# A two-layer recurrent model in one kernel: zeros of a parked image written from a tile on chip, large products of a block inversion moved to GpSimd, the first two heads inverted on TensorE, and a new order of all work

## The chip, the cores and the metric

One core of a Trainium2 chip runs the whole program in one launch. The metric is the device time of that launch in microseconds. Engines are called TensorE (PE in the rows, PEld for its weight loads), VectorE (DVE), ScalarE (ACT), GpSimd (POOL) and SyncE (SP), which issues nearly all DMAs here.

## The reference

Two layers over x of shape (2, 512, 256). Layer 0 multiplies causal attention (16 heads of 16) with silu of a mixture of 8 experts. Layer 1 is the larger part: 16 key heads, each with two value heads, a delta rule with decay, and beside it a mixture with 2 shared and 16 routed experts (top 2). Cut to what matters:

```python
def step(state, inp):                      # layer 1, for each token t
    q_t, k_t, v_t, b_t, d_t = inp
    Sk = jnp.einsum('bhi,bhipj->bhpj', k_t, state)
    delta = (v_t - Sk) * b_t[..., None]
    upd = jnp.einsum('bhi,bhpj->bhipj', k_t, delta)
    state = state * d_t[:, :, None, :, None] + upd
    o = jnp.einsum('bhi,bhipj->bhpj', q_t, state)
    return (state, o)
...
s = _L1_attn_ref(xn, ...)                  # conv of 4 taps, the scan, rmsnorm, silu(z), W_out
g = _silu(_L1_ffn_ref(xn, ...))
x = x + s * g
```

## The kernel before

**Chunks.** The scan is done in chunks of 128 tokens. A unit u (0 to 63) is one chunk i of one key head h, u = 4h + i, for both batches and both value heads: four lanes of 128x128. Inside a chunk the delta rule needs the inverse of a lower triangular 128x128 matrix, one for each lane. The kernel inverts it by doubling: from the inverses of the diagonal blocks of width w those of width 2w are made.

**The steps of a unit**, by the names of the plan: `row` and `dec` fetch and build the decays (RC, E; SP, GpSimd, ScalarE), `gram` multiplies keys and queries (TensorE L1580) and masks them on VectorE (L2200: M for the inverse, PTE for the output), `pl` and `pm` (GpSimd L2754, L2758, L2760) split M into a high and a low 16-bit part in the tile LM and put ones on the diagonal. `ls` stores LM into an image in memory called `parked` (two buffers, one for each second head), `ps` and `pd` take PTE through memory to transpose its place.

**The inner blocks, once for each head.** When the four units of a head are parked, `dg` loads their 16x16 diagonal blocks into LC (eight DMAs), so that each partition holds blocks of its own. `iv1`, `iv2`, `iv3` invert them there on VectorE in sixteen small instructions; the last four are a product of 512 elements (L1909, `times_left`), a sum (L2223), a product of 512 (L1915, `times_right`) and a sum (L2229). ScalarE copies the result and its transpose to 16 bits (`xc`), and `sx` stores it back into the image in sixteen DMAs (L1253). The rest of the image's inverse planes must be zero: that is what the two `blank` transfers of the start are for.

**The outer levels, for each unit.** `ld` loads the unit's inverse, its transpose and its matrix, high and low (XYLM, three buffers, L1260). Then for levels k = 5, 6, 7: `a` (TensorE L1591, four matmuls of 64 columns, then VectorE L2238 masks into ZL) and `b` (TensorE L1600 and L1603, eight such matmuls, then ScalarE L2516 writes back into XYLM). `r` and `c` refine the result once and give W (VectorE L2244, L2252). The state recurrence follows: `KS`, `U`, `so` (TensorE L1630, L1646, L1660), normalisation `sq`, `on`, gating `ot`, and the output products `os`, `ol`, `y`, `yl`.

**Other work** fills the engines: the projections and the convolution of the next heads (`ck`, `cq`, `cv`, `Zt`: products L1307 on TensorE, taps L2116 on VectorE), `fWK`, `fWV`, `fWO` (weights, split by GpSimd into a high and a low part), the routing (`top`, `cnt`, `own`, `tiles`, `hits`) and the experts.

**Order.** Every engine runs a fixed list in order. The lists come from a planner at build time (`Plan.arrange`): each part has an engine, a cost and the parts it comes after; of the parts ready, the one with the earliest start (in steps of `GRAIN`) goes first, and ties go by a rank. `RANK` and `LATER` shift ranks and starts for each kind of part and engine; they were searched.

**The start of the program.** SP fetches weights; the transfers of the small inputs (`fetch_small`) all count on one semaphore:

```python
for k in range(2):
    sp.dma_start(parked[k, 0:2].rearrange("k p q t -> k p (q t)").bitcast(U16),
                 A["blank"].unsqueeze(0).broadcast_to((2, 128, 2048))).then_inc(d_l1, 16)
...
elif x[0] == "spg":                       # GpSimd: the split of wab (L2586, L2588)
    w.wait_ge(d_l1, 96)
```

`spg` stands in GpSimd's list between splits of expert weights (`fx`, tiles exh and exl). Behind it come two `fWK` and three `fx`.

Of the kernel before, what the change touches and what calls it, by code (L numbers as in the profile page):

```python
# [18 lines left out]
D = 256  # L19
NT = 8  # L20
C_ID, C_SEL, C_U, C_ONE, C_LV = 0, 128, 256, 384, 512
LEVELS = range(5, 8)
C_IO = C_LV + 3 * 64
# [12 lines left out]
def constants():  # L36
# [21 lines left out]
def later_keys():  # L58
# [16 lines left out]
    "KS": {"ACT": -190.92, "DVE": -1855.73, "PE": -624.17}, "KS:first": {"ACT": 227.91, "DVE": -29.25, "PE": 1091.89},  # L75
    "KS:last": {"ACT": 19.9, "DVE": -251.47, "PE": -182.36}, "U": {"ACT": 271.82, "PE": -704.74},
    "U:first": {"ACT": 522.41, "PE": -459.55}, "U:last": {"ACT": 1098.98, "PE": 26.26},
    "Vt": {"ACT": 1966.37, "PE": 1.01}, "Vt:first": {"ACT": -177.22, "PE": 116.15},
    "Zt": {"ACT": -442.91, "DVE": 372.72, "PE": 0.27}, "Zt:first": {"ACT": -6.92, "DVE": -918.91, "PE": 0.43},
    "a": {"DVE": 745.93, "PE": -37.51}, "a:first": {"DVE": 7.23, "PE": -43.11},  # L80
    "a:last": {"DVE": 219.97, "PE": -2044.99}, "am:0": {"POOL": -319.97}, "am:1": {"POOL": -358.83},
    "b": {"ACT": 1147.73, "PE": -216.88}, "b:first": {"ACT": -284.84, "PE": -11.2},
    "b:last": {"ACT": 1292.06, "PE": -123.68}, "c": {"DVE": 139.61, "PE": -193.02},
    "c:first": {"DVE": 5.13, "PE": -513.63}, "c:last": {"DVE": -88.29, "PE": 203.76},
    "cb": {"DMA": 35.71, "DVE": -174.03, "POOL": -432.42}, "ck": {"ACT": -69.56, "PE": -8.56}, "ck1": {"DVE": -77.72},
    "ck1:first": {"DVE": -32.49}, "ck2": {"DVE": 1249.32}, "ck2:first": {"DVE": -735.45}, "ck3": {"DVE": 2346.47},
    "ck3:first": {"DVE": 71.49}, "ck:first": {"ACT": 60.74, "PE": -13.19}, "cnt": {"DVE": 69.46, "PE": 259.48},
    "cq": {"ACT": -622.29, "PE": 0.48}, "cq1": {"DVE": 113.6}, "cq1:first": {"DVE": -39.01}, "cq2": {"DVE": 2640.45},
    "cq2:first": {"DVE": 206.34}, "cq3": {"DVE": -540.73}, "cq3:first": {"DVE": 677.48},
    "cq:first": {"ACT": -297.9, "PE": -14.62}, "crow": {"ACT": 48.35, "PE": -275.28, "SP": 352.22},  # L90
# [3 lines left out]
    "dd:1": {"SP": 438.02}, "dec": {"ACT": -84.12, "POOL": -63.05}, "dec:first": {"ACT": 152.18, "POOL": -5.94},  # L94
    "dec:last": {"ACT": -310, "POOL": -684.57}, "dg": {"SP": -106.09}, "dg:first": {"SP": -251.24},
# [2778 lines left out]
```

## Time and profile before

| | us |
|---|---|
| median of 3 runs | 1363.14 |
| lowest, highest | 1357.52, 1367.53 |
| the profiled execution | 1364.12 |
| its span, first to last instruction | 1362.4 |

| engine | busy us | share of the span |
|---|---|---|
| TensorE | 1173.1 | 86% |
| TensorE, weight loads | 981.3 | 72% |
| VectorE | 1101.6 | 81% |
| ScalarE | 833.0 | 61% |
| GpSimd | 823.1 | 60% |

The share is a mean over stages: layer 0 (to about 280 us), the prologue and the filling of layer 1's pipeline (to about 450), the steady part over 16 heads, and the tail. Matmuls are pipelined and their ends are modelled, so TensorE's busy time is not its peak. The profile also gives the clock that TensorE was granted, as a share of full speed, here 0.946 in the mean.

### The profile page before, as it was taken

The numbers are of one execution on the slowest core, as the hardware profiler recorded it, in microseconds if no ns is written. First come the engines' busy times: TensorE is split into PE (matmuls) and PEld (weight loads), VectorE is DVE, ScalarE is ACT, GpSimd is POOL, SyncE is SP. The second block draws the span as 40 slices with busy tenths as digits, with TensorE's granted clock in tenths as the row PEclk, the third lists the DMA queues.
The fourth block names the chain that finished last, engine by engine and source line by source line (L and its number), as shares of the span: only waits on it lengthen the run. The fifth ranks groups of instructions, "written<-read, shape, count | busy, mean of one in ns | idle before, by whom it ended". The sixth has DMA issues, their size and how long they took to land.

```text
span 1362.4 us, 28169 instructions
## 1 busy us (share of the span) xinstructions
PE 1173.1 (86%) x9546; PEld 981.3 (72%) x9546; DVE 1101.6 (81%) x2393; ACT 833.0 (61%) x2377; POOL 823.1 (60%) x1052
## 2 busy tenths in 40 slices
PE   9890997979288899899889998999998999988996
PEld 7560544658177788879778887888886888877885
DVE  6790523698889889798988898899888988977888
ACT  4000364267266677677757785777776677857675
POOL 3111244255765587777587776876776778666636
PEclk9895798989699999999999998999999999989998
DMA  7931011315354364653566444644463654554442
GB/s 224 234 110 56 16 53 40 96 62 143 87 165 128 97 163 126 172 156 108 140 155 188 111 128 114 176 116 141 107 196 86 171 151 134 138 128 122 132 123 67
DMA packets 236871, 172.41 MB, mean 127 GB/s; under 512 B 116824, under 2 KB 204120, under 8 KB 236696
## 3 DMA queue, kind: packets, MB, share of 16 engines
q1 hardware_dynamic: 231992, 156.32, 42.0%
q0 software_dynamic: 4736, 14.29, 3.9%
q8 instruction: 77, 1.26, 0.4%
q14 instruction: 66, 0.54, 0.1%
HBM read 121.93 MB, written 50.52 MB: 127 GB/s over the span
## 4 chain that ended last, share of the span: by engine, by line
PE 28%; DVE 24%; DMA 20%; SPq 9%; POOL 8%; issue 7%; ACT 4%; DVEq 0%; POOLq 0%; ACTq 0%
PE ps L1307 10%; DMA XYLM<-parked 6%; SPq L1253 4%; DMA parked<-LM 4%; DMA parked<-in_blank 3%; SPq L1245 3%; DVE yv L2116 3%; DVE KQ L2116 2%; DVE PR L1909 2%; DVE PR L1915 2%; DMA RC<-crow 2%; DMA LC<-parked 2%; POOL LM L2758 1%; DMA parked<-XY 1%; DVE M L2200 1%
## 5 line engine op out<-in xcount | busy, mean ns | idle before, releaser
L2116 DVE SCALAR_TENSOR_TENSOR KQ<-ps,cw,KQ 128x511 f32<-128x511 f32 (+2 forms) x192 | 141.2, 743 | 6.6 <-ACT KQ L2452 4.1
L2116 DVE SCALAR_TENSOR_TENSOR yv<-ps,cw,yv 128x511 f32<-128x511 f32 (+2 forms) x192 | 142.5, 744 | 3.5
L2516 ACT ACTIVATE XYLM<-ps 128x512 f16<-128x512 f32 x192 | 111.2, 598 | 52.5 <-PE ps L1603 49.7
L1307 PE MATMUL ps<-XH,WVh 128*128 128x256 f32 (+1 forms) x384 | 135.6, 353 | 4.6 <-ACT QSc L2525 2.0
L2550 ACT ACTIVATE sq<-O 128x128 bf16<-128x128 f32 x256 | 79.3, 310 | 75.5 <-DVE O L2288 32.1
L1307 PE MATMUL ps<-XH,WVl 128*128 128x256 f32 (+1 forms) x384 | 124.2, 324 | 0.0
L1307 PE MATMUL ps<-XL,WVh 128*128 128x256 f32 (+1 forms) x384 | 124.1, 323 | 0.0
L2238 DVE TENSOR_TENSOR ZL<-ps,cst 128x256 f16<-128x256 f32 x192 | 78.0, 418 | 20.8 <-PE ps L1591 17.3
L2744 POOL TENSOR_TENSOR RC<-RC,dec 128x512 f32<-128x512 f32 x64 | 67.7, 1057 | 32.1 <-DMA RC<-crow 31.9
L2556 ACT ACTIVATE O<-O,small 128x128 f32<-128x128 f32 x256 | 82.4, 410 | 3.0 <-POOL small L2770 2.6
L1995 DVE TENSOR_REDUCE Mp<-ps 128x2 f32<-128x768 f32 (+2 forms) x64 | 48.8, 816 | 43.0 <-PE ps L1387 42.8
L2380 ACT ACTIVATE hT<-ps 128x512 f32<-128x512 f32 x16 | 9.6, 598 | 120.7 <-PE ps L1307 120.7
L2789 POOL TENSOR_TENSOR OGL<-O,OGH 128x512 fp32r<-128x512 f32 x62 | 80.2, 1294 | 5.1
L1307 PEld LDWEIGHTS ps<-XH,WVh 128*128 128x128 f32 x384 | 74.1, 193 | 10.4 <-ACT QSc L2525 2.7
L1630 PE MATMUL ps<-S,KQ 128*128 128x256 f32 x192 | 62.4, 407 | 20.8 <-DVE O L2288 13.4
L2758 POOL TENSOR_TENSOR LM<-M,LM 128x512 f16<-128x512 f32 x64 | 76.6, 1198 | 5.2
L1660 PEld LDWEIGHTS ps<-De,PT 128*128 128x128 f32 x512 | 74.4, 191 | 6.3 <-ACT De L2541 0.9
L1307 PEld LDWEIGHTS ps<-XH,WVl 128*128 128x128 f32 x384 | 73.6, 192 | 6.0
L1660 PE MATMUL ps<-De,PT 128*128 128x128 f32 x512 | 77.1, 275 | 0.8 <-ACT De L2541 0.6
L1307 PEld LDWEIGHTS ps<-XL,WVh 128*128 128x128 f32 x384 | 74.3, 194 | 3.8
L2538 ACT ACTIVATE D<-ps,dec 128x128 f32<-128x128 f32 x192 | 60.8, 376 | 25.2 <-PE ps L1646 24.9
L1591 PE MATMUL ps<-XYLM 128*128 128x64 f16 x768 | 51.5, 195 | 27.2 <-DMA XYLM<-parked 24.6
(341 smaller groups left out, 4123.5 us busy)
## 6 DMA issues: line engine op xcount, KB each, us to landing
XYLM<-parked SPq DMA_DIRECT2D x64, 512.0 KB, 5.4
RC<-crow SPq DMA_DIRECT2D x128, 128.0 KB, 4.8
decayed<-PTE SPq DMA_DIRECT2D x64, 256.0 KB, 4.4
PT<-decayed SPq DMA_DIRECT2D x64, 256.0 KB, 3.3
parked<-LM SPq DMA_DIRECT2D x64, 256.0 KB, 3.5
WV<-in_WV SPq DMA_DIRECT2D x16, 512.0 KB, 3.7
exr<-in_ex SPq DMA_DIRECT2D x16, 384.0 KB, 5.9
WK<-in_WK SPq DMA_DIRECT2D x16, 256.0 KB, 2.9
```

What stands on the lines that cost most here:

```text
L1307: m = pe.matmul(o, a, b, start=c + k == 0, stop=c == 1 and k == 2)
L1630: pe.matmul(ps[:, bk, 0:256], K[:, h % 3, 128 * n:128 * n + 128], S[:, b], start=True, stop=True)
L1660: m = pe.matmul(ps[:, bk, 256 + 128 * v:384 + 128 * v], PT[:, u % 2, 2 * b + v, :], De[:, b, v, :], start=True, stop=True)
L2116: m = dve.scalar_tensor_tensor(out=dst[:, k:512], in0=ps[:, bk, 0:512 - k], scalar=cw[:, h, j, 3 - k:4 - k], in1=dst[:, k:512], op0=ALU.mu ...
L2238: leave(dve.tensor_tensor(half(ZL[:, k - 5], k, 0), p, lv(k), ALU.mult), "a", u, k)
L2516: leave(act.activation(changed(u, k), ps[:, bank("b", u, k), :].rearrange("p (c n t) -> p c n t", c=2, t=1 << (k - 1)), ACT.Copy), "b", u, k)
L2538: m = act.activation(D2[:, b, v, :], ps[:, bk, 128 * v:128 * v + 128], ACT.Copy, scale=bE[:, cl:cl + 1])
L2550: act.activation(sq[:, 1, :], O[:, u % 2, l, :], ACT.Square, accum_out=so[:, u % 2, l:l + 1]).then_inc(s_sqo, 1)
L2556: m = act.activation(O[:, u % 2, l, :], O[:, u % 2, l, :], ACT.Copy, scale=ro[:, u % 2, l:l + 1])
L2744: pool.tensor_tensor(rc.rearrange("p (b v) t -> p b v t", b=2), rc.rearrange("p (b v) t -> p b v t", b=2), bias.unsqueeze(3).broadcast_to( ...
L2758: pool.tensor_tensor(early(u, 1), M[:, u % 2], early(u, 0), ALU.subtract).then_inc(s_ml, 1)
L2789: pool.tensor_tensor(OGL[:], O[:, u % 2], OGH[:].bitcast(F32), ALU.subtract).then_inc(s_ogl, 1)
```

## The change

1. The zeros of the image come from a tile `blank` (128 x 512, 16 bits) that GpSimd clears at the start, in four DMAs of 512 KB with the 128 partitions outermost, instead of two DMAs of 1 MB from an input in memory with the two buffers outermost. All waits on the semaphore go from 96 to 128.
2. The two products of 512 elements of a head's inner blocks are issued by GpSimd (`p8`, `q8`) instead of VectorE; the sums stay.
3. The first two heads (`LEAD`, eight units, `OWN`) don't go through memory. GpSimd writes their masks straight into XYLM, adds the transposed first step (`py`) and the identity (`xi`), TensorE and VectorE do a first step `x1`, and the doubling runs from level 2 to 7 instead of 5 to 7. For them `ls`, `dg`, `iv`, `xc`, `sx` and `ld` fall away. The masks of levels 2 to 4 lie in a tile ZF that shares its place with XC and PR, so `iv1` of head 2 waits for level 4 of all eight units; `pl`, `py`, `xi` of unit u wait for the unit three before, since XYLM has three buffers.
4. The planner's costs of SP are the issue alone, and landings are parts of their own; `RANK` and `LATER` are new throughout, so all lists are in a new order.

```diff
-C_ID, C_SEL, C_U, C_ONE, C_LV = 0, 128, 256, 384, 512
-LEVELS = range(5, 8)
+C_ID, C_SEL, C_U, C_ONE, C_X1, C_Y1, C_LV = 0, 128, 256, 384, 512, 576, 704
+LEVELS = range(2, 8)
+OUTER = 5
+LEAD = 2
+OWN = 4 * LEAD
...
-    P.add(("pt", u), rank + 0.1, ("DVE", 0.79, (("gram", u), "DVE"), earlier(2, "ps", "SP")), gives=("gram", u))
-    P.add(("ps", u), rank + 0.2, ("SP", 1.0, (("pt", u), "DVE"), earlier(8, "pd", "SP")))
+    P.add(("pt", u), rank + 0.1, ("DVE", 0.79, (("gram", u), "DVE"), earlier(2, "ps", "DMA")), gives=("gram", u))
+    P.add(("ps", u), rank + 0.2, ("SP", 0.45, (("pt", u), "DVE"), earlier(8, "pd", "DMA")), ("DMA", 1.5))
+    if u < OWN:
+        rank = u - 1.5
+        P.add(("pl", u), rank, ("POOL", 0.6, (("gram", u), "DVE"), earlier(3, "c", "DVE"), earlier(3, "r", "PE")))
+        P.add(("pm", u), rank, ("POOL", 2.1, (("pl", u), "POOL")))
+        P.add(("py", u), rank + 0.1, ("POOL", 1.2, (("pm", u), "POOL")))
+        P.add(("xi", u), rank, ("POOL", 0.48, earlier(3, "r", "PE"), (("cc", 1), "POOL")))
+        P.add(("x1", u), rank + 0.2, ("PE", 0.12, (("pm", u), "POOL"), (("cc", 1), "POOL")),
+              ("DVE", 0.34, earlier(3, "r", "PE"), (("xi", u), "POOL")), takes=True, gives=("x1", u))
+        return
...
-    P.add(("iv2", h), rank + 0.1, ("DVE", 1.3, (("iv1", h), "DVE")))
-    P.add(("iv3", h), rank + 0.1, ("DVE", 1.3, (("iv2", h), "DVE")))
+    P.add(("p8", h), rank + 0.1, ("POOL", 1.15, (("iv1", h), "DVE")))
+    P.add(("iv2", h), rank + 0.1, ("DVE", 0.8, (("p8", h), "POOL")))
+    P.add(("q8", h), rank + 0.1, ("POOL", 1.15, (("iv2", h), "DVE")))
+    P.add(("iv3", h), rank + 0.1, ("DVE", 0.8, (("q8", h), "POOL")))
...
+        first_head = ExitStack()
+        ZF = sb("ZF", [128, 3, 4, 128], F16, scope=first_head)
+        first_head.close()
         XC = sb("XC", [128, 256])
         PR = sb("PR", [128, 512])
...
-                for k in range(2):
-                    sp.dma_start(parked[k, 0:2].rearrange("k p q t -> k p (q t)").bitcast(U16),
-                                 A["blank"].unsqueeze(0).broadcast_to((2, 128, 2048))).then_inc(d_l1, 16)
+                w.wait_ge(s_c0, 2)
+                for k in range(4):
+                    sp.dma_start(parked[k // 2, k % 2].rearrange("p (a q) t -> p a (q t)", a=4),
+                                 blank[:].unsqueeze(1).broadcast_to((128, 4, 512))).then_inc(d_l1, 16)
...
+                elif what == "x1":
+                    u = x[1]
+                    bk = enter(*x)
+                    w.wait_ge(s_const, 2)
+                    w.wait_ge(s_one, nth("POOL", "pm", u))
+                    for l in range(4):
+                        m = pe.matmul(ps[:, bk, 64 * l:64 * l + 64], xy(u, 2)[:, l, :], half(id16[:], 1, 0), start=True, stop=True)
+                    signal(m, *x)
...
                 elif what == "iv1":
                     h = x[1]
-                    w.wait_ge(d_dg, 128 * (h + 1))
-                    if h:
-                        w.wait_ge(s_xc, 2 * h)
-                    inner_blocks(IV * h)
+                    w.wait_ge(d_dg, 128 * (h - LEAD + 1))
+                    if h > LEAD:
+                        w.wait_ge(s_xc, 2 * (h - LEAD))
+                    else:
+                        for u in range(OWN):
+                            w.wait_ge(*full("b", u, OUTER - 1))
+                    inner_blocks(IV * (h - LEAD))
...
+                elif x[0] == "p8":
+                    h = x[1]
+                    w.wait_ge(s_iv, IV * (h - LEAD) + 12)
+                    times_left(pool, 8, 0, PR[:])
+                elif x[0] == "q8":
+                    h = x[1]
+                    w.wait_ge(s_iv, IV * (h - LEAD) + 14)
+                    times_right(pool, 8, 0, 0, PR[:])
                 elif x[0] == "pl":
                     u = x[1]
                     w.wait_ge(s_m, nth("DVE", "gram", u))
-                    if u > 1:
-                        w.wait_ge(d_ls[u % 2], 16 * ((u - 2) // 2 + 1))
+                    if u >= OWN + 2:
+                        w.wait_ge(d_ls[u % 2], 16 * ((u - 2 - OWN) // 2 + 1))
+                    elif 2 < u < OWN:
+                        w.wait_ge(*done("c", u - 3))
...
+                elif x[0] == "xi":
+                    u = x[1]
+                    w.wait_ge(s_const, 2)
+                    if u > 2:
+                        w.wait_ge(*full("r", u - 3))
+                    pool.tensor_copy(half(xy(u, 0), 1, 1), half(spread4(id16[:]), 1, 1)).then_inc(s_xi, 1)
+                elif x[0] == "py":
+                    u = x[1]
+                    w.wait_ge(s_one, nth("POOL", "pm", u))
+                    if u > 2:
+                        w.wait_ge(*done("c", u - 3))
+                    pool.tensor_tensor(xy(u, 1), xy(u, 2), spread4(cst[:, C_Y1:C_Y1 + 128]), ALU.mult).then_inc(s_y1, 1)
```

## Rows read from the trace of the kernel before

**Rows 1.** the page: TensorE and VectorE (busy us, share, instructions), TensorE by slices

```profile
PE 1173.1 (86%) x9546; PEld 981.3 (72%) x9546; DVE 1101.6 (81%) x2393; ACT 833.0 (61%) x2377; POOL 823.1 (60%) x1052
...
PE   9890997979288899899889998999998999988996
```

**Rows 2.** the chain that ended last, in order of time: start us, us, what

```profile
89.78 41.44 DMA parked<-in_blank
...
338.21 4.77 DMA parked<-LM
...
368.88 5.18 DMA XYLM<-parked
...
376.86 0.23 PE ps L1591 x4
...
378.96 0.29 PE ps L1591 x4
...
433.89 0.13 PE ps L1600 x4
```

**Rows 3.** the waits: engine line waited for, us in total, times, longest

```profile
POOL wabh L2586 <- DMA parked<-in_blank: 40.7, 1, 40.7
...
PE ps L1591 <- DMA XYLM<-parked: 24.6, 18, 2.3
...
PE ps L1530 <- issue: 23.5, 1, 23.5
...
PE ps L1630 <- DVE O L2288: 13.4, 11, 3.9
```

**Rows 4.** timeline near the pause: start us, us, engine, line, what

```profile
89.06 1.33 SPq L1113 DMA_DIRECT2D parked<-in_blank  x2
...
131.28 0.32 POOL L2586 CAST wabh<-wab 128x160 fp32r<-128x160 f32 x1 [40.73 <-DMA parked<-in_blank]
...
138.02 0.76 PE L1307 MATMUL ps<-XH,exh 128*128 128x512 f32 x1 [34.40 <-POOL exl L2588]
```

**Rows 5.** windows: stretch, length, engines busy, clock, DMA share, GB/s

```profile
core 0: us, PE busy (x) PEld busy (x) DVE busy (x) ACT busy (x) POOL busy (x), PEclk, DMA share, GB/s
88.00:92.00 4.00, 3.86 (x30) 2.52 (x30) 3.69 (x8) 0.00 (x0) 1.89 (x2) 1.00 1.06 314
104.00:131.00 27.00, 0.00 (x0) 0.00 (x0) 1.36 (x4) 0.00 (x0) 0.00 (x0) 0.52 0.12 54
131.00:160.00 29.00, 20.88 (x110) 12.22 (x114) 11.59 (x18) 7.75 (x11) 11.21 (x14) 0.62 0.03 7
335.00:380.00 45.00, 17.34 (x140) 14.21 (x139) 39.61 (x101) 14.84 (x38) 32.16 (x43) 0.70 0.48 130
335.00:600.00 265.00, 214.87 (x1868) 187.09 (x1868) 232.52 (x529) 169.26 (x513) 190.04 (x241) 0.94 0.50 135
600.00:1200.00 600.00, 556.62 (x4928) 493.26 (x4927) 538.22 (x1149) 434.95 (x1318) 434.15 (x552) 0.99 0.52 141
```

**Rows 6.** the page's DMA issues: times, KB each, median us from issue to landing

```profile
parked<-LM SPq DMA_DIRECT2D x64, 256.0 KB, 3.5
```

**Rows 7.** timeline of unit 0: its masks on GpSimd, its W on VectorE

```profile
317.43 0.61 POOL L2754 CAST LM<-M 128x512 f16<-128x512 f32 x1 [2.55 <-DVE M L2200]
...
383.24 0.68 DVE L2252 SCALAR_TENSOR_TENSOR W<-ps,XYLM 128x512 f32<-128x512 f32 x1
```

**Rows 8.** groups by form on TensorE: busy us, mean ns of one

```profile
L1600 PE MATMUL ps<-ZL,XYLM 128*128 128x64 f16 x768 | 54.2, 196 | 9.5 <-DVE ZL L2238 9.2
```

**Rows 9.** groups by form on VectorE and GpSimd

```profile
L2238 DVE TENSOR_TENSOR ZL<-ps,cst 128x256 f16<-128x256 f32 x192 | 78.0, 418 | 20.8 <-PE ps L1591 17.3 <-PE ps L1603 2.0 <-issue 0.9
...
L1915 DVE TENSOR_TENSOR PR<-XC,ZC 128x512 f32<-128x512 f32 x16 | 22.7, 1417 | 0.0
L1909 DVE TENSOR_TENSOR PR<-XC 128x512 f32<-128x512 f32 x16 | 19.5, 1218 | 0.2
...
L2758 POOL TENSOR_TENSOR LM<-M,LM 128x512 f16<-128x512 f32 x64 | 76.6, 1198 | 5.2
```

More of the change, by code:

```diff
@@ L74 @@
 RANK = {
[L75 to L90, printed above, removed]
[3 rows of a table removed]
@@ new lines @@
+    "sc:1": {"ACT": 0.5}, "sd": {"DVE": 0.15}, "slot": {"DVE": 0.08}, "small": {"SP": 0.53}, "so": {"DVE": 0.04},
+    "so:first": {"PE": 0.15}, "sq": {"POOL": 1.41}, "sq:first": {"ACT": 2.13, "POOL": 0.12},
+    "sq:last": {"ACT": 0.82, "POOL": 3.7}, "sr": {"DMA": 1.97, "POOL": 2.33}, "ss": {"SP": 0.87}, "su": {"ACT": 1.89},
+    "sw": {"DMA": 1.13, "POOL": 0.91}, "sx": {"DMA": 0.16}, "tiles": {"DVE": 3.89}, "tn0": {"DVE": 0.38},
+    "top": {"ACT": 0.01, "DVE": 1.9}, "tp": {"ACT": 1.34, "DVE": 1.51}, "up": {"ACT": 1.73}, "x1": {"DVE": 0.24},
@@ L179, with levels @@
-UNITS = ("row", "dec", "gram", "pt", "pl", "pm", "ls", "ps", "ld", "pd", "a", "b", "r", "c", "KS", "U", "so", "sq", "on", "ot", "os", "ol", "y", "yl")
+HEADS = ("ck", "ck1", "ck2", "ck3", "cq", "cq1", "cq2", "cq3", "cv", "cv1", "cv2", "cv3", "kn", "kb", "kns", "Vt", "Zt", "dg", "iv1", "p8", "iv2", "q8", "iv3", "xc", "sx")
+UNITS = ("row", "dec", "gram", "pt", "pl", "pm", "py", "xi", "x1", "ls", "ps", "ld", "pd", "a", "b", "r", "c", "KS", "U", "so", "sq", "on", "ot", "os", "ol", "y", "yl")
+def levels(u):
+    return LEVELS if u < OWN else range(OUTER, 8)
@@ L501, in plan_chunk @@
+    P.add(("pl", u), rank + 0.1, ("POOL", 0.6, (("gram", u), "DVE"), earlier(2, "ls", "DMA") if u > OWN + 1 else None))
     P.add(("pm", u), rank + 0.1, ("POOL", 2.1, (("pl", u), "POOL")))
-    P.add(("ls", u), rank + 0.2, ("SP", 1.0, (("pm", u), "POOL"), earlier(8, "ld", "SP")))
+    P.add(("ls", u), rank + 0.2, ("SP", 0.45, (("pm", u), "POOL"), earlier(8, "ld", "DMA") if u > OWN + 7 else None), ("DMA", 0.8))
 def plan_blocks(P, h):
     rank = 4 * h - 3.8
-    units = [(("ls", 4 * h + i), "SP") for i in range(4)]
@@ L508, in plan_blocks @@
-    P.add(("dg", h), rank, ("SP", 4.0, *units, (("iv1", h - 1), "DVE") if h else None))
-    P.add(("iv1", h), rank + 0.1, ("DVE", 2.5, (("dg", h), "SP"), (("xc", h - 1), "ACT") if h else None))
-    P.add(("iv2", h), rank + 0.1, ("DVE", 1.3, (("iv1", h), "DVE")))
-    P.add(("iv3", h), rank + 0.1, ("DVE", 1.3, (("iv2", h), "DVE")))
-    P.add(("xc", h), rank + 0.2, ("ACT", 0.9, (("iv3", h), "DVE"), (("sx", h - 1), "SP") if h else None))
-    P.add(("sx", h), rank + 0.2, ("SP", 8.0, (("xc", h), "ACT")))
+    units = [(("ls", 4 * h + i), "DMA") for i in range(4)]
@@ new lines, in plan_blocks @@
+    P.add(("dg", h), rank, ("SP", 4.0, *units, (("iv1", h - 1), "DVE") if h > LEAD else None), ("DMA", 0.3))
+    P.add(("iv1", h), rank + 0.1, ("DVE", 3.6, (("dg", h), "DMA"), (("xc", h - 1), "ACT") if h > LEAD else None,
+                                   *([(("b", k, OUTER - 1), "PE") for k in range(OWN)] if h == LEAD else [])))
+    P.add(("p8", h), rank + 0.1, ("POOL", 1.15, (("iv1", h), "DVE")))
+    P.add(("iv2", h), rank + 0.1, ("DVE", 0.8, (("p8", h), "POOL")))
+    P.add(("q8", h), rank + 0.1, ("POOL", 1.15, (("iv2", h), "DVE")))
@@ L665, in plan1 @@
         plan_chunk(P, u)
-    for h in range(HK):
+    for h in range(LEAD, HK):
         plan_blocks(P, h)
```

282 lines of the change are left out of this document (159 added, 123 removed), and 34 rows, old and new, of tables (LATER, RANK).

## The prediction

> **What bounds the kernel now.** I read the page first [rows 1]. TensorE is busy 86% of the span and VectorE 81%, and the row of slices has one hole: in the fourth slice (102 to 136 us) TensorE is at 0 and everything else nearly so. The page's chain of waits, in order of time [rows 2], names the hole: one piece of 41.44 us, the transfer of zeros into the parked image, which starts at 89.78. The waits [rows 3] say who stood there: GpSimd, 40.7 us, ahead of the split of wab (L2586), because that split waits for all six small loads and both zero transfers on one semaphore. GpSimd runs its list in order, and behind that instruction stand the splits of the experts' weights. So TensorE stops at 104 and starts again at 138.02 after 34.40 us [rows 4]. By stages [rows 5]: nothing runs in 104 to 131; from 335 to 380 TensorE is busy 17.3 of 45 us; over 600 to 1200 it is busy 556.6 of 600 (92.8%), VectorE 538.2 (89.7%), GpSimd 434.2 (72.4%). So there are three different limits: a wait (104 to 138), a fill of the second layer's pipeline (335 to 380), and then two engines that are both nearly full.
>
> The fill's limit stands in the chain too [rows 2]: the mask of the fourth unit goes out at 338.21 (4.77 us), eight short loads bring its blocks, VectorE inverts, sixteen short stores write the blocks back, and the image comes in in 5.18 us from 368.88. TensorE sits 23.5 us in one piece there, nominally before the routing count L1530 [rows 3], but the image for the first level landed only at 374.1, so the count's wait cost nothing.
>
> **The change, part by part.** The sum is made against the profiled execution, 1364.12 us with a span of 1362.4; the median of the three runs is 1363.14, about a microsecond lower, which I ignore. A measurement of this kernel can tell about 1% from no change (the three runs lie 1357.52 to 1367.53).
>
> *Zeros from a tile.* The two transfers of 1 MB each (128 rows of 4 KB, the two buffers as outermost dimension) become four of 512 KB with the 128 partitions outermost. In 104 to 131 the core's 16 DMA engines were busy 0.12, so about 1.9 engines worked, and 54 GB/s moved [rows 5]; in 88 to 92, with loads of ordinary shape, it was 314 GB/s. At that rate 2.1 MB take 6.7 us. What lies ahead of them on the queue (bo, wo, wab, rows, cw, two WK: 1.4 MB by the shapes) takes 4.5 us more at the most. The nearest store of the new shape is that of the masks, parked<-LM, 256 KB in pieces of 1 KB with a median of 3.5 us from issue to landing [rows 6]; eight of them one after the other would be 28 us, the upper end, at full overlap 7. Between these I take the rate, since the queue's entries overlap in the rows of 88 to 92: issue at 89.1, landing at 99 (97 to 103). The GpSimd wait then ends at 99 instead of 131.28 [rows 4]: 32 us. The wait that is late next is the experts' weights themselves: three loads of 384 KB are queued behind the zeros, 1.2 MB, 4 us more, so about 103. GpSimd meanwhile does wab and the two WK splits as it did from 131.28 to 135.9 (4.6 us), so the load is hidden to within a microsecond. Gain 32, bounds 26 and 34 (the whole of TensorE's pause). The added memset of one tile is on GpSimd ahead of its first weights.
>
> The trace alone gives the ends of that sum. The Trainium skill, page "DMA: Bandwidth & Descriptors", section "Rules for kernel authors", says why the old shape was slow and that the new one is not: an outermost dimension of c below 16 confines a transfer to c engines, 128 partitions outermost use all 16. The share of 0.12 agrees with two engines; that the new shape gets sixteen no row here shows. By that rule alone the sum would be the one I took.
>
> *Clock.* While TensorE stood, its granted clock fell to 0.52, which is the lower of its two levels (1.2 of 2.4 GHz), and it came back late: 0.62 in 131 to 160, where it was busy 20.88 us; it was 1.00 in 88 to 92 [rows 5]. At 1.00 that work is 12.9 us. If the pause goes, 8 us go at most; nothing if the thin products of the scores let it fall anyway. I take 5.
>
> *First two heads on TensorE alone.* For the eight units of heads 0 and 1 the trip through memory goes (masks out, blocks in, VectorE's inversion, blocks out, image in), and levels 2 to 4 and a first step x1 come in. The masks of unit 0 are ready at 317.43 + 2.65 = 320.1 [rows 7]. A level took from 376.86 to 378.96, 2.1 us [rows 2]: six levels 12.6, with py 1.2 and x1 0.6 before and r, c 2.5 after them, 17 us: unit 0's W at about 337 instead of 383.9 (L2252, first at 383.24 [rows 7]). That is latency and not time won: what can be won is what the engines can fill. Over 335 to 600 TensorE was busy 214.9 of 265; at the 92.8% of later it would have been 245.9, so 31 us are idle beyond the ordinary. The added products cost, by issue to issue, 4 matmuls in 0.13 us (the piece at 433.89 [rows 2]), three such groups a level, 24 levels and eight x1: 10 us; by busy time 0.27 to 0.28 a group (54.2 us for the 768 matmuls of L1600, 192 groups [rows 8]; the other two kinds are within 3 us of it): 22 us. So TensorE allows a gain of 31 - 11 = 20 down to 31 - 24 = 7. VectorE: an inversion of one head costs it 7.5 us (its fourteen kinds of instruction take 120.7 us in 16 heads; the two largest are in [rows 9]); two of them go, 15.1; 32 operations of 418 ns come in, 13.4; three more heads in this stretch lose 2.6 each (next part), 7.9. It had 232.5, it will have 223, at its later 89.7% 248 us instead of 265: 17. I take 12, bounds 0 (what fills the stretch is then the chain, not the engines) and 20. GpSimd's added py (1.2, as L2758 [rows 9]), xi (0.5) and three casts of ZF (0.6 each) are 16 us where it was busy 190 of 265; they lie on it beside other work. What is late next is VectorE's list: iv1 of head 2 now waits for level 4 of all eight units (the tiles overlap), and pl of units 3 to 7 waits for c three units back.
>
> *Products of 512 on GpSimd.* Two per head, L1909 and L1915 in their 512 form, 19.5 + 22.7 = 42.2 us in 16 heads, 2.64 a head [rows 9]; for 14 heads 36.9 us leave VectorE. GpSimd's nearest row of the same size, LM, is 1198 ns [rows 9]; I take 1.2, 34 us in all on an engine at 72%. The chain of each head gets two hand-offs longer and may stand behind a GpSimd operation of 1.3 us twice: up to 3.4 us a head. It matters only where the image is the last to come: TensorE's wait for it (L1591) is 24.6 us in 18 of 192 cases [rows 3]. What VectorE's 3% can give back is bounded by TensorE's waits on it: 13.4 us for O at L1630 [rows 3], and about as much again at its other lines, 30 us in the whole second layer at the most. I take a fifth, 6; bounds -10 (a share of 14 x 3.4) and +20.
>
> Here a rule speaks against the change. VectorE's own 512 products are the same work at L1909 and L1915, and took 1218 and 1417 ns in the mean [rows 9]; an ordinary 256-element product takes it 418, so 512 would be 0.8 to 0.9: they wait for something. The Trainium skill, "SBUF — State Buffer", section "Who interferes with whom", has it that a VectorE instruction with two operands in SBUF contends with a GpSimd instruction that reads it, and the loser stands. By that rule moving the product moves the contention too. By rows: if each moved product is stretched as on VectorE, by up to 0.5 us, 28 x 0.5 = 14 us more on GpSimd, which its 28% of idle time covers; the sum stays.
>
> *Order.* All ranks are new and the planner now knows SP's issue and the landing apart. What it can win is inside the last two parts; I price it at 0 beyond them, with 8 us either way for a new order of some 28000 instructions.
>
> *Sum:* 1364 - 32 - 5 - 12 - 6 = 1309; I say 1310.
>
> **The rivals.**
> (a) The fill does not shorten: the gram of units 5 to 7 waits on masks that wait on c, VectorE's one-off routing work (it was busy 39.6 of 45 in 335 to 380 [rows 5]) takes the room. For it: VectorE, not TensorE, was full there. Against: 10 of these 39.6 were head 0's inversion. Time 1364 - 32 - 3 - 0 = 1329, between 1322 and 1342.
> (b) VectorE's relief and the order give much more: TensorE to 96% in 600 to 1200 (-20), all 20 of the fill, clock 7: 1364 - 34 - 7 - 20 - 17 = 1286.
> (c) Slower: the inversion's chain becomes the bound of every head. Place: from the last mask of a head to its image, now with two GpSimd turns in it. Price: 3.4 us x 14 = 48, and no gain of the fill or of VectorE: 1364 - 32 - 5 + 48 = 1375. It decides from the point where every head's image is the last to arrive at level 5; 18 of 192 now, so against it stands the slack of nine levels in ten.
> (d) The zeros are written by few engines again, or something else holds GpSimd's list there: 1364 - 12 - 6 = 1346 with the rest as forecast.
>
> **How the numbers follow.** The forecast, 1296 to 1322: 0.52. (a) 0.23. (b) 0.17. (c) 0.03. (d) 0.05. The predicted time is the first's, 1310. The range takes in most of (a) and the nearer part of (b): 1284 to 1335. Below 1350 (faster by over 1%) lie all but (c) and a part of (d): 0.94; within 1% 0.04; slower 0.02.
>
> **What will show it.** The chain piece of 41 us is gone, GpSimd's wait at the split of wab is under 10 us, and TensorE's pause near 104 is under 5 us with the clock staying at 1.00; the experts' part ends some 37 us earlier. First W some 40 us or more before the place it would have (383 - 37 = 346), so near 305, and TensorE's busy share in the 45 us before it above 0.6. VectorE's busy time is 1101.6 - 37 - 15 + 13 = 1063 [rows 1], GpSimd's 50 more than it was. The prediction is wrong if TensorE has a new idle stretch around iv1 of head 2 or pl of units 3 to 7, if the experts' loads land later than the zeros let them, or if the 92.8% of 600 to 1200 has fallen.

## The result, and the profile after

| | us |
|---|---|
| changed kernel, median of 3 | 1290.69 |
| kernel before, median of 4 | 1360.33 |
| ratio, 95% interval | 0.949 (0.941 to 0.957) |
| spans of the profiled executions | 1288.9 after, 1362.4 before |

The kernel became 5.1% faster, 70 us by the medians and 73.5 us by the two spans. The forecast was 1310 with a range of 1284 to 1335. A fourth run of the changed kernel, at 1438 us, fell in the chip's slow state (granted clock 0.744 against 0.965 to 0.972 in the others) and is left out.

The page of the changed kernel, the lines that answer to [rows 1]:

```profile
PE 1176.2 (91%) x9866; PEld 987.2 (77%) x9866; DVE 1062.3 (82%) x2365; ACT 841.6 (65%) x2393; POOL 869.4 (67%) x1101
...
PE   8899889788986999998999899989999999899996
```

The hole of the fourth slice is gone. TensorE's busy time is 3.1 us longer, in a span that is 73.5 us shorter. VectorE has 39.3 us less (forecast 38.6), and GpSimd 46.3 us more (forecast 50).

Its timeline near the zeros and at the first W, to set beside [rows 4] and [rows 7]:

```profile
88.89 4.10 SPq L1165 DMA_DIRECT2D parked<-blank  x4
...
98.73 0.32 POOL L2646 CAST wabh<-wab 128x160 fp32r<-128x160 f32 x1 [2.28 <-DMA parked<-blank]
...
318.97 0.68 DVE L2312 SCALAR_TENSOR_TENSOR W<-ps,XYLM 128x512 f32<-128x512 f32 x1
```

The split of wab starts at 98.73, where it started at 131.28 (forecast 99). GpSimd waited 2.28 us for the zeros, not 40.7, because the new order also does the two WK splits first. The first W starts at 319, 64 us before its old time; I had said 78 (near 305).

The windows of the same stretches as in [rows 5]; the fill's stretch is shifted:

```profile
core 0: us, PE busy (x) PEld busy (x) DVE busy (x) ACT busy (x) POOL busy (x), PEclk, DMA share, GB/s
104.00:131.00 27.00, 25.90 (x180) 15.21 (x178) 19.99 (x38) 13.88 (x21) 6.82 (x9) 1.00 0.09 23
131.00:160.00 29.00, 24.88 (x174) 11.69 (x172) 6.05 (x14) 16.41 (x28) 12.98 (x17) 0.94 0.19 58
340.00:385.00 45.00, 40.61 (x446) 33.44 (x445) 41.07 (x89) 30.44 (x76) 33.29 (x44) 1.00 0.36 97
...
600.00:1200.00 600.00, 568.41 (x5024) 506.33 (x5022) 524.57 (x1156) 449.05 (x1349) 468.43 (x591) 0.99 0.52 144
```

In 104 to 131 TensorE is busy 25.9 of 27 us at clock 1.00, where it stood still at 0.52. The 45 us after 340 show 40.6 us of TensorE, where 335 to 380 showed 17.3. And in 600 to 1200 TensorE is busy 568.4 us, 94.7%, against 92.8% [rows 5], with VectorE at 87.4% in place of 89.7%.

The moved products, by form (busy, mean ns of one, then idle time of GpSimd ahead of them):

```profile
L1017 POOL TENSOR_TENSOR PR<-XC,ZC 128x512 f32<-128x512 f32 x14 | 22.1, 1580 | 14.6 <-DVE ZC L2276 14.6
L1011 POOL TENSOR_TENSOR PR<-XC 128x512 f32<-128x512 f32 x14 | 21.3, 1520 | 7.6 <-DVE XC L1996 7.6
```

They take 1.52 and 1.58 us, not the 1.2 that I priced from LM [rows 9]: 43.4 us in all, not 34.

A mark near the end of layer 0 splits the gain: `crow`, the store of the decay rows, with which SP starts the second layer. Timeline of SP, before and then in the changed kernel:

```profile
303.24 0.37 SPq L1216 DMA_DIRECT2D crow<-RC  x1
```

```profile
262.18 0.36 SPq L1268 DMA_DIRECT2D crow<-RC  x1
```

So 41.1 us are won ahead of that point, and 32.4 us behind it, in these two profiles. The first part was forecast at 37, the second at 18.

### The profile page after: what moved, and what is told of

It is laid out like the page before. It is cut to its first block, busy times and chain, and to the rows that moved or that the text cites. A ratio compares the mean times of both kernels' runs of the same rounds, so it can differ in the third digit from the quotient of the medians.

```text
span 1288.9 us, 28774 instructions
## 1 busy us (share of the span) xinstructions
PE 1176.2 (91%) x9866; PEld 987.2 (77%) x9866; DVE 1062.3 (82%) x2365; ACT 841.6 (65%) x2393; POOL 869.4 (67%) x1101
## 4 chain that ended last, share of the span: by engine, by line
PE 39%; DVE 19%; POOL 10%; DMA 10%; issue 8%; ACT 7%; SPq 5%; DVEq 0%; POOLq 0%; another core or an unknown queue 0%; ACTq 0%
PE ps L1359 12%; DMA XYLM<-parked 4%; SPq L1305 4%; DVE yv L2168 3%; DMA WK<-in_WK 3%; PE ps L1757 3%; DVE KQ L2168 2%; PE ps L1421 2%; PE ps L1632 2%; PE ps L1694 1%; PE ps L1724 1%; PE ps L1710 1%; PE ps L1765 1%; PE ps L1467 1%; DVE Mp L2047 1%
## 5 line engine op out<-in xcount | busy, mean ns | idle before, releaser
L2576 ACT ACTIVATE XYLM<-ps 128x512 f16<-128x512 f32 x216 | 125.3, 600 | 54.7 <-PE ps L1667 54.0
L1653 PE MATMUL ps<-XYLM 128*128 128x64 f16 x864 | 57.5, 194 | 18.2 <-DMA XYLM<-parked 12.7
L2585 ACT ACTIVATE QSc<-ps,dec 128x128 f32<-128x128 f32 x192 | 58.7, 369 | 23.4 <-DVE RH L2324 23.0
L1632 PE MATMUL ps<-KQ 128*128 128x256 f32 x256 | 70.4, 398 | 2.7 <-ACT XYLM L2576 0.7
L2854 POOL TENSOR_TENSOR small<-small 128x4 f32<-128x4 f32 (+1 forms) x66 | 67.7, 1025 | 5.5
L1757 PE MATMUL ps<-WOh,OGH 128*128 128x256 f32 x248 | 67.0, 303 | 4.4 <-POOL OGH L2867 3.5
```

The source lines that it names most:

```text
L1632: m = pe.matmul(ps[:, bk, 256 * b:256 * b + 256].rearrange("p (k t) -> p k t", k=2), K[:, h % 3, at], KQ[:, h % 3, :, at], start=True, sto ...
L1757: pe.matmul(ps[:, bk, 256 * b:256 * b + 256], OGH[:, 2 * b + v, :], weights[:, h % 2, v, :], start=v + k == 0, stop=False, skip_group_chec ...
L2576: leave(act.activation(changed(u, k), ps[:, bank("b", u, k), :].rearrange("p (c n t) -> p c n t", c=2, t=1 << (k - 1)), ACT.Copy), "b", u, k)
L2854: pool.tensor_tensor(ro[:, u % 2, four], ro[:, u % 2, four], mh[:, four], ALU.pow).then_inc(s_ro, 1)
```

## The experiments

Ratios are to runs of the kernel before on the same chip, whose medians were 1358, 1347 and 1349 us in the three batches, against 1360 beside the changed kernel, which was not run again. So a difference from the changed kernel is given twice: by the medians, and by the ratios. The second takes out the difference between chips, and is uncertain by some 13 us either way, by the 95% intervals. The profiles of kernels with the same lists ahead of `crow` put it at times up to 5.5 us apart, so lengths of the second layer are counted from each profile's own `crow`.

### 1. Zeros from the tile alone

```diff
 # the kernel before, all lists unchanged; also: tile blank, its memset, waits 96 -> 128
-                for k in range(2):
-                    sp.dma_start(parked[k, 0:2].rearrange("k p q t -> k p (q t)").bitcast(U16),
-                                 A["blank"].unsqueeze(0).broadcast_to((2, 128, 2048))).then_inc(d_l1, 16)
+                w.wait_ge(s_c0, 2)
+                for k in range(4):
+                    sp.dma_start(parked[k // 2, k % 2].rearrange("p (a q) t -> p a (q t)", a=4),
+                                 blank[:].unsqueeze(1).broadcast_to((128, 4, 512))).then_inc(d_l1, 16)
```

> The kernel before with the zeros from the tile alone, all lists as before. If the zeros and the clock are the step that I priced (32 + 5), this gives 1360 - 37 = 1323, ratio 0.973, and the first decay row store (crow) that stood at 303.2 us comes at 263 to 267. If the second layer had slack that swallows an earlier start, the end moves by less than the crow does. If the new order of the start had a part in the 41 us by which crow moved in the changed kernel, crow moves by clearly less than 41 here.

Measured: 1327.6, ratio 0.977 (0.970 to 0.983). Timeline of GpSimd and SP in this kernel:

```profile
97.85 0.32 POOL L2588 CAST wabh<-wab 128x160 fp32r<-128x160 f32 x1 [8.42 <-DMA parked<-blank]
...
267.00 0.37 SPq L1218 DMA_DIRECT2D crow<-RC  x1
```

`crow` comes 36.2 us earlier, 37 were priced. The end of the span comes 33.7 us earlier, and the median is 31 us below that of the kernel before. So the zeros give 31 to 36 of the 73.5 us. The 4.8 us that are left of the 41.1 ahead of `crow` are less than the 5.5 us between like profiles, so one pair of profiles can't give them to the new lists.

### 2. Zeros from memory, rows outermost

```diff
 # the kernel before
-                    sp.dma_start(parked[k, 0:2].rearrange("k p q t -> k p (q t)").bitcast(U16),
-                                 A["blank"].unsqueeze(0).broadcast_to((2, 128, 2048))).then_inc(d_l1, 16)
+                    sp.dma_start(parked[k, 0:2].rearrange("k p q t -> p k (q t)").bitcast(U16),
+                                 A["blank"].unsqueeze(1).broadcast_to((128, 2, 2048))).then_inc(d_l1, 16)
```

> The kernel before; the zeros still come from memory in two transfers, but with the 128 rows outermost and the two buffers second. If the old shape (outermost dimension of 2, so two DMA engines) was the cause, this gains as much as the zeros from the tile, within 3 us: 1323. If the source in memory was the cause, it stays at 1360.

Measured: 1323.7, ratio 0.976 (0.970 to 0.982). The DMA issues in 88 to 104 of this kernel (times, KB each, median us from issue to landing):

```profile
parked<-in_blank SPq DMA_DIRECT2D x2, 1024.0 KB, 9.0
```

The same megabytes from the same place land in 9.0 us, where they took 41.4 in the chain of the kernel before [rows 2]. The order of the dimensions was the cause, and the source was not. The tile was not needed for this gain.

### 3. The products back on VectorE

```diff
 # the changed kernel, all lists unchanged
                 elif what == "iv2":
                     h = x[1]
+                    w.wait_ge(s_iv, IV * (h - LEAD) + 12)
+                    times_left(dve, 8, 0, PR[:])
...
                 elif x[0] == "p8":
-                    h = x[1]
-                    w.wait_ge(s_iv, IV * (h - LEAD) + 12)
-                    times_left(pool, 8, 0, PR[:])
+                    pass
 # and the same for iv3 and q8
```

> The changed kernel, every list as it is, but the two products of 512 elements of heads 2 to 15 issued by VectorE again, in front of their sums. My theory: VectorE gains 37 us of work and the end comes 6 us later (0 to 15), 1297. Rival: since the lists were searched for GpSimd, VectorE's relief is worth much more, 20 us or more. Other rival: the hand-offs cost what the relief gives, within 3 us of the changed kernel.

Measured: 1313.8, ratio 0.968 (0.963 to 0.974), behind the changed kernel by 23 us by the medians and by 26 us by the ratios, which fits the rival. By form on VectorE the products are:

```profile
L1017 DVE TENSOR_TENSOR PR<-XC,ZC 128x512 f32<-128x512 f32 x14 | 17.7, 1264 | 0.0
L1011 DVE TENSOR_TENSOR PR<-XC 128x512 f32<-128x512 f32 x14 | 16.6, 1185 | 0.0
```

That is 34.3 us in 28 instructions, and 23 to 26 us reach the end.

### 4. The products on GpSimd, in the lists of before

```diff
 # the kernel of experiment 1; products of all 16 heads
+        for h in range(HK):            # after the planner is done, into GpSimd's list alone
+            for new, old in (("p8", "iv1"), ("q8", "iv2")):
+                at = when[(old, h), "DVE"][1]
+                k = next((n for n, x in enumerate(order["POOL"]) if when[x, "POOL"][0] >= at), len(order["POOL"]))
+                order["POOL"].insert(k, (new, h))
```

> The kernel before with the zeros from the tile (1327.5 when run) and the two products of 512 elements on GpSimd for all 16 heads; every list stays, the products are inserted in GpSimd's list at the place of the planned end of the step before. If VectorE's relief is worth the 22 us that its loss cost in the changed kernel, this gives 1305. If that 22 us was a matter of lists fitted to the products' place, this gives 1320 to 1335. My first price was 6: 1321.

Measured: 1327.9, ratio 0.984 (0.979 to 0.990), against 0.977 (0.970 to 0.983) for the same kernel without the move: no gain, perhaps a small loss. The products in it (min, median, max ns; then who waited for them, us and times):

```profile
L981 POOL TENSOR_TENSOR PR<-XC x16: 1465/1500/1531, 321.2 to 1245.7; 128x512 f32<-128x512 f32 x16
...
L987 POOL TENSOR_TENSOR PR<-XC,ZC x16: 1466/1512/1624, 324.9 to 1248.4; 128x512 f32<-128x512 f32 x16
...
  DVE ZC L2230: 26.6, 16
...
  DVE XC L2234: 14.5, 10
```

All sixteen first sums waited for their product, 26.6 us together, and ten of the second sums for theirs, 14.5 us. In the changed kernel the same two waits are (who waited, us, times):

```profile
  DVE ZC L2276: 4.9, 5
...
  DVE XC L2280: 1.8, 4
```

In lists that were not made for it, the move takes 42 us of work from VectorE, and VectorE stands 41 us for what was moved; in the changed kernel it stands 6.7.

### 5 and 6. More work on one engine, off the chain

Both keep the changed kernel's lists. GpSimd's products stay as they are, and the products are computed once more into the tile of zeros, and nobody reads that.

```diff
 # 5: on VectorE, ahead of its sums
                 elif what == "iv2":
+                    w.wait_ge(s_iv, IV * (h - LEAD) + 12)
+                    times_left(dve, 8, 0, blank[:], False)
 # 6: on GpSimd, behind the one that is used
                     times_left(pool, 8, 0, PR[:])
+                    w.wait_ge(s_c0, 2 + 2 * (h - LEAD))
+                    times_left(pool, 8, 0, blank[:], False)
 # and the same for times_right
```

> The changed kernel, GpSimd's products as they are, and VectorE computes both products of 512 once more into the tile of zeros (used up by then), in front of its sums; nobody reads the copies. 28 more instructions of 1.2 to 1.4 us on VectorE. If VectorE's load is what the products' return to VectorE cost (22 us), this costs 15 to 25 us: 1306 to 1316 where the changed kernel has 1291. If that cost was the place of the product in the chain and not the load, this costs under 8.

> The changed kernel, and GpSimd computes each of the two products of 512 a second time into the tile of zeros, behind the one that is used. 28 more instructions of about 1.5 us, 43 us, on GpSimd, none of them in the chain of the inversion except that the second product may wait 0.6 us for the first copy. If GpSimd's idle time covers such work, as I wrote, this costs under 6 us (1291 to 1297). If GpSimd is by now as near to the bound as VectorE, it costs 15 us or more.

Measured: on VectorE 1310.3, ratio 0.970 (0.966 to 0.975); on GpSimd 1313.2, ratio 0.972 (0.967 to 0.977). The copies, by form, on VectorE and on GpSimd:

```profile
L1019 DVE TENSOR_TENSOR blank<-XC,ZC 128x512 f16<-128x512 f32 x14 | 17.4, 1245 | 0.0
L1011 DVE TENSOR_TENSOR blank<-XC 128x512 f16<-128x512 f32 x14 | 16.2, 1160 | 0.0
```

```profile
L1018 POOL TENSOR_TENSOR blank<-XC,ZC 128x512 f16<-128x512 f32 x14 | 21.7, 1548 | 0.0
...
L1011 POOL TENSOR_TENSOR blank<-XC 128x512 f16<-128x512 f32 x14 | 21.3, 1524 | 0.0
```

33.6 us more on VectorE cost 20 us by the medians and 28 by the ratios. 43.0 us more on GpSimd cost 23 and 30 us: my sentence that GpSimd's 28% of idle time covers such work is wrong. The two costs are alike, from half of the work added to over four fifths of it, although one engine was busy 87% and the other 78% of 600 to 1200. That doesn't yet show that each added microsecond costs its share. Experiment 7 adds no work at all, and loses nearly as much against the searched kernel as these two. So the runs do not separate the load on an engine from the loss of the fit that the search had found between lists and durations; adding half as much work, or much less, might.

### 7 and 8. Other lists for the same work

One planner cost, that of the copy `xc`, is changed from 1.1 to 1.2 and to 1.0. The planner makes other lists: with 1.2 from two fifths of each compute engine's list on (TensorE's first difference is at `ot` of unit 17), with 1.0 from a little over a quarter on (`a` of unit 9).

> The changed kernel; one planner cost of ScalarE (the copy xc) is 1.2 in place of 1.1, so all lists from about unit 11 on come out otherwise, with the same work and unsearched. If a list made by the same rules is worth as much as the searched one, 1291 within 5. If the search itself is a term of the gain, it is slower by that term: I expect 5 to 20 us, 1296 to 1311, all of it after 400 us.

> The changed kernel with the planner's cost of the copy xc at 1.0 in place of 1.1: a third list of the same work. The second list gave a ratio of 0.969 against the searched one's 0.949. If 2% is what an unsearched list costs, this gives 0.960 to 0.980; if it lies at 0.95, the searched list is not special; above 0.99, lists scatter by more than the parts of the change that I try to price.

Measured: 1306.3, ratio 0.969 (0.966 to 0.973), which is behind the changed kernel by 16 us by the medians and 27 by the ratios; and 1402.9, ratio 1.040 (1.034 to 1.045). The third list is 9 points behind the searched one, with the same instructions. In it the largest wait of TensorE for the image, of 600 to 1401 (us, times, longest):

```profile
PE ps L1653 <- DMA XYLM<-parked: 36.5, 5, 18.3
```

Five waits for the image of an inverse, one of them 18.3 us: in this list the chain of a head does end last at places, as my rival (c) had it.

### 9. The new structure with the old tables

RANK and LATER of the kernel before, everything else as changed.

> The changed kernel with the planner's two tables of shifts (RANK and LATER) of the kernel before, so the new structure and costs without the new search. My theory (structure carries the gain): 1291 + 10 = 1300 to 1310. Rival (the search made the 20 us that I missed): 1315 or more. If unsearched lists are simply bad it could be over 1330, and then it says only that tables and structure have to fit.

Measured: 1373.6, ratio 1.012 (1.006 to 1.018). Without tables that fit, the whole change comes out 1.2% slower than the kernel before. My own forecast of 1300 to 1310 for this run was far off, and the gain can't be put down to the structure alone.

### 10 to 12. None or one of the heads on TensorE alone

```diff
-LEAD = 2
+LEAD = 0        # 10
+LEAD = 1        # 11; 12 also: LATER of tiles 3.89 -> 0, of hits 1.67 -> 0
```

> The changed kernel with LEAD = 0: no head inverted on TensorE alone, all sixteen through memory; tables unchanged, lists planned anew. If the two heads are worth the 12 us that I gave them, this is 12 us above a re-planned list of the changed kernel (the run with the other list), so about 1315 to 1320. If, as the units show (their lead of 27 us over the kernel with zeros alone is gone at unit 10), they are worth nothing, it is within 5 us of that run. The fill (TensorE's busy time in the 113 us after the crow store) should fall from 96 to near 79 us in both cases.

> The changed kernel with LEAD = 1: only head 0 on TensorE alone. If the gain of the fill comes from the first head's trip through memory (36 us of chain), this is as fast as LEAD = 2 re-planned, within 5 us. If the second head matters as well, it lies half-way to LEAD = 0.

> LEAD = 1 as before, and the planner's shifts of the routing steps tiles and hits set to 0, so that the first gather of the routed experts stands at place 216 of GpSimd's list (415 in LEAD = 1 before, 200 in the changed kernel). If LEAD = 1 was slow only because its routed experts came late (they began at 832 us and held the last 80 us of the run), this gives 1291 to 1310, and the second head is worth little. If the second head is worth as much as the first, it stays above 1330.

Measured: LEAD = 0 1381.5, ratio 1.024 (1.020 to 1.029); LEAD = 1 1371.4, ratio 1.016 (1.010 to 1.021); with earlier routing 1345.7, ratio 0.997 (0.994 to 0.999). The fill of LEAD = 0 (window 267 to 380; TensorE is the third number):

```profile
267.00:380.00 113.00, 57.60 (x394) 46.20 (x395) 80.55 (x192) 41.31 (x90) 80.99 (x100) 0.74 0.52 133
```

57.6 us, not the 79 that I expected for both. The gathers of the routed experts (min, median, max ns, first and last start), first in LEAD = 1, then with earlier routing:

```profile
L2749 POOL DMA_INDIRECT st<-xnd,toki x31: 946/989/1112, 832.0 to 1326.5; - x31
```

```profile
L2749 POOL DMA_INDIRECT st<-xnd,toki x31: 959/1077/1113, 500.0 to 1050.5; - x31
```

In LEAD = 1 the first gather starts at 832, and the last at 1326.5, in the tail of the run; in the changed kernel they run from 462 to 1140. With a start at 500 the kernel is 26 us faster, in what is again another list, and it is still 4.7 points behind LEAD = 2. Since the lists of one and the same structure lie 9 points apart (experiments 7 and 8), these three runs can't price a head. They show only that each setting of LEAD needs tables of its own.

## Why the prediction was right, step by step

The range held, and the point was 19 us too high: 54 us of gain were forecast, and 70 came. The result, 1291, lies below the 1296 to 1322 that had the chance of 0.52. It lies in the stretch between that and rival (b), and only the bounds took it in. The part ahead of `crow` was forecast by its mechanism; the part behind it was not.

**Zeros and clock (37, bounds 26 and 42).** Shown, and sized within the scatter: 36.2 us at `crow`, 33.7 at the end of the span, 31 by the medians. The split of wab, forecast for 99, started at 97.9 in experiment 1 and at 98.7 in the changed kernel, and the clock row of 104 to 131 is 1.00 in the changed kernel. Of the 36.2 us, 33.4 are the earlier start of that split (131.28 to 97.85). The 2.8 us that are left for the clock are inside the 5.5 us between like profiles, so my 5 us for it are not shown by themselves. TensorE's pause ended when GpSimd had split the experts' weights, and GpSimd stood at the split of wab until 131.28. But that wait was not the only one that held it. The load of the experts' weights issued just behind the zeros (window 90 to 92 of the kernel before; times, KB, us to landing) was late too:

```profile
exr<-in_ex SPq DMA_DIRECT2D x1, 384.0 KB, 41.2
```

It was issued at 90.91 and landed at 132.1, after the zeros. A change that only let `spg` wait for fewer transfers would therefore have left most of the pause, by this row; no run tried it. The rule that I had from the Trainium skill, "DMA: Bandwidth & Descriptors", section "Rules for kernel authors", is what experiment 2 bears out: two outermost copies 41.4 us, 128 rows outermost 9.0.

**Fill (12, bounds 0 and 20).** The mechanism is there, but the gain was mis-sized. In 274 to 319, the 45 us before the first W, TensorE is busy 33.4 us, a share of 0.74 (I had said above 0.6). Windows from `crow` to the end, then two stretches of the fill, first the kernel with zeros alone and then the changed one:

```profile
267.00:1328.70 1061.70, 947.09 (x8126) 833.34 (x8124) 928.99 (x2025) 731.82 (x2197) 733.89 (x932) 0.96 0.50 134
267.00:380.00 113.00, 78.98 (x583) 66.42 (x582) 99.59 (x233) 63.63 (x162) 75.06 (x98) 0.87 0.50 126
380.00:500.00 120.00, 109.71 (x937) 95.76 (x935) 102.91 (x226) 82.03 (x259) 83.26 (x109) 0.94 0.49 132
600.00:1200.00 600.00, 558.13 (x4803) 493.11 (x4802) 534.43 (x1154) 431.76 (x1309) 434.29 (x549) 0.97 0.52 139
```

```profile
262.20:1288.90 1026.70, 943.05 (x8428) 832.98 (x8426) 890.06 (x2002) 741.47 (x2208) 774.99 (x970) 0.98 0.48 133
267.00:380.00 113.00, 96.22 (x960) 80.11 (x958) 92.59 (x202) 75.72 (x185) 79.95 (x105) 0.95 0.33 89
380.00:500.00 120.00, 104.25 (x880) 92.40 (x880) 108.15 (x275) 79.36 (x257) 98.24 (x122) 0.96 0.49 132
```

In 267 to 380 TensorE has 17.2 us more work done, in 380 to 500 5.5 us less. The 11.7 us that remain are about the 10 to 22 us of products that the change itself adds. The start of head 2's inversion says the same. XC<-LC is its first instruction (durations, then first and last start; the second line is head 2's in the kernel with zeros alone), again that kernel first:

```profile
L1922 DVE TENSOR_SCALAR XC<-LC x16: 390/408/1317, 311.1 to 1244.3; 128x256 f32<-128x256 f16 x16
...
421.10 0.40 DVE L1922 TENSOR_SCALAR XC<-LC 128x256 f32<-128x256 f16 x1 [2.85 <-DMA LC<-parked]
```

```profile
L1972 DVE TENSOR_SCALAR XC<-LC x14: 379/406/1890, 411.6 to 1206.4; 128x256 f32<-128x256 f16 x14
```

Head 2 starts at 411.6, where it started at 421: 9 us earlier, 5 of them won already at `crow`. From its own `crow` head 2 starts after 149.4 us in the changed kernel, and after 153.7 to 158.3 in the kernel before and in experiments 1, 2 and 4. So the first two heads by themselves were worth about 4 us by then, 9 at the most, and not 12. (The bounds of 7 and 20 us that I gave from TensorE took off 24 and 11 us for added products which the text puts at 22 and 10; that moves them by 1 to 2 us.) Rival (a) named the place rightly: the early W (27 us ahead of the kernel with zeros alone) did not carry to head 2, and the chain of the changed kernel passes GpSimd's masks and weight splits and waits for WK there (from 369 to 392).

**Products on GpSimd (6, bounds -10 and 20), and the order (0, 8 either way).** Here is the missing part. The product of 512 was itself priced too low (34 us on GpSimd, 43.4 measured), which alone would have made the gain smaller and not larger. From head 2 to head 15 the inversions of the changed kernel start every 61.1 us ((1206.4 - 411.6) / 13), those of the kernel with zeros alone every 63.3 us ((1244.3 - 421) / 13): 2.2 us a head, 29 in all. TensorE's idle time from `crow` to the end fell from 1061.7 - 947.1 = 114.6 to 1026.7 - 943.1 = 83.6 us, 31 of the 35 us between these two stretches.

How far one profile can be trusted here, experiment 2 tells, which has the same lists as the kernel with zeros alone:

```profile
270.20:1322.50 1052.30, 943.62 (x8128) 831.12 (x8126) 925.96 (x2026) 732.55 (x2198) 737.20 (x932) 0.96 0.50 135
```

```profile
428.56 0.39 DVE L1920 TENSOR_SCALAR XC<-LC 128x256 f32<-128x256 f16 x1 [2.49 <-DMA LC<-parked]
```

It is 9.4 us shorter from `crow` to the end, with 108.7 us of idle TensorE, and its heads start every 62.3 us ((1238.0 - 428.6) / 13). So the gain behind `crow` is 26 to 35 us, and the faster pace 1.1 to 2.2 us a head, 15 to 29 us in all.

With the products back on VectorE (experiment 3) the idle time is

```profile
264.00:1316.40 1052.40, 951.49 (x8428) 836.89 (x8427) 923.28 (x2030) 742.05 (x2208) 743.25 (x942) 0.98 0.48 129
```

1052.4 - 951.5 = 100.9 us, and the heads start every 62.9 us:

```profile
L1972 DVE TENSOR_SCALAR XC<-LC x14: 379/394/1883, 413.7 to 1230.8; 128x256 f32<-128x256 f16 x14
```

The step that failed is the pricing of the two as separate terms, each from its own row: 6 us for the products by TensorE's waits, and 0 for the order. In their place the runs show 15 to 29 us for both together. In the old lists the move gains nothing, since VectorE then stands 41 us for the products (experiment 4). In the new ones it stands 6.7 us, and taking the move back costs 23 to 26 us (experiment 3). New lists without a search lose from 2 to 9 points (experiments 7 to 9). Experiment 3 does not price the relief alone either, since experiment 7, with the products left on GpSimd, loses nearly as much (16 to 27 us). How the 15 to 29 us divide between the relief and a search that would also have found something without it stays open: that needs a search for the old structure with its zeros mended, which was not tried.

**GpSimd's cover.** Wrong, as experiment 6 shows: GpSimd had 28% of idle time, and the end came 23 to 30 us later. These two rows, from the profile's own `crow` to the end, are the copies on GpSimd and then the copies on VectorE; TensorE's idle time grew to 102.2 and 95.5 us:

```profile
267.10:1316.20 1049.10, 946.92 (x8429) 833.64 (x8427) 891.93 (x2002) 741.29 (x2209) 815.49 (x998) 0.98 0.47 130
```

```profile
262.50:1309.50 1047.00, 951.53 (x8428) 835.39 (x8426) 919.99 (x2030) 740.88 (x2208) 786.54 (x970) 0.98 0.47 130
```

The second list of the same work, with nothing added (experiment 7), has 92 us, and is as long from `crow` to the end as the copies on VectorE:

```profile
264.10:1311.20 1047.10, 954.98 (x8428) 840.61 (x8426) 891.07 (x2002) 740.95 (x2209) 772.26 (x970) 0.98 0.47 130
```

**The rule on shared access.** VectorE's products, which took 1218 and 1417 ns in the mean [rows 9], took 1185 and 1264 in experiment 3, and 1160 and 1245 as copies, with the longest near 2 us; GpSimd's own stay between 1.47 and 1.71 us in every run. The Trainium skill, "SBUF — State Buffer", section "Who interferes with whom", would have the one that comes second wait; the spread on VectorE's side agrees with that, and the narrow band on GpSimd's shows no such waiting there. The shortest copy took 1.01 us, so the 0.8 to 0.9 us that I took for a product that waits for nothing was too low. No run here isolates what the waits cost at the end.

**The other rivals.** (b), 1286, lay nearest to the result, for a part of its reasons. TensorE's 94.7% in 600 to 1200 is on the way to the 96 that it had said. The 20 us of the fill and the 7 us of the clock, which its sum also needs, were not found, so its nearness is partly luck. (It prices the 96% at 20 us and puts 17 into its sum.) (c), the longer chain, did not come about: TensorE waited for the image in the changed kernel (waits: us, times, longest)

```profile
PE ps L1653 <- DMA XYLM<-parked: 12.7, 9, 4.4
```

against 24.6 us [rows 3]; experiment 8 shows it in a bad list. The slack that I set against (c), 18 waits in 192, was misread: of a unit's three levels only level 5 needs the image, so it was 18 in 64, and is 9 in 56 now. (d) fell with GpSimd's wait of 2.28 us for the zeros. Of my three signs of a wrong forecast one is there in a small way: in 385 to 412, ahead of head 2's inversion, TensorE is idle 8.0 of 27 us, at a clock of 0.87. The other two are not: the split of exr behind that of wab found its weights landed, and 600 to 1200 rose.

## What to carry to other kernels

When all engines stop together, follow the waits back to the instruction that is held, look what its semaphore counts, and read the shape of the transfer behind it and the landings of the loads queued after it. An outermost dimension of 2 cost 31 to 36 us here, and turning two dimensions mended it (experiment 2). In a kernel whose engines run long fixed lists, an edit can't be priced apart from its lists. Moving work off a nearly full engine gave nothing in the old lists, and taking it back cost 23 to 26 us in lists searched for it, so compare structures only after the same search for each. Don't count idle time in such lists as a cover: half or more of what was added to either engine came out at the end.

## What the runs showed of the hardware that I had not expected

The two products of 512 elements, whose operands are broadcast and strided views, take GpSimd 1.52 and 1.58 us in the mean, longer than subtractions of contiguous operands of the same size: 1.20 us for LM [rows 9], 1.28 us for exl. Broadcasting alone doesn't make the difference: in the kernel before, the sum for RC, also 512 elements and with one operand broadcast, took 1.06 us. Nor does the type of the output: the copies of experiment 6 write 16 bits and took 1.52 and 1.55 us. Which of the other traits does it, no run isolates.

The two zero transfers of 1 MB, with about two DMA engines at work (0.12 of 16 [rows 5]), did not only take 41 us themselves: the weight loads issued behind them were late as well. The loads of exr issued in 84 to 140 (times, KB each, median us from issue to landing), in the kernel before, in experiment 2 and in the changed kernel:

```profile
exr<-in_ex SPq DMA_DIRECT2D x4, 384.0 KB, 35.1
```

```profile
exr<-in_ex SPq DMA_DIRECT2D x6, 384.0 KB, 3.7
```

```profile
exr<-in_ex SPq DMA_DIRECT2D x7, 384.0 KB, 3.9
```

They took 35.1 us to land with the old zeros ahead of them, and 3.7 in experiment 2, where only the shape of the zeros differs and the same megabytes stand ahead of them.
